# A local-attention layer stack on one core: attention weights turned on VectorE, score heads on partition quarters, group transposes in 64-row pieces, and a new static order

## The chip, the cores and the metric

The program runs on one core of a Trainium2 chip. Its time is the device time of one execution in microseconds (us). Five engines work side by side, each on its own list of instructions in a fixed order: TensorE (PE, with its weight loads PEld), VectorE (DVE), ScalarE (ACT), GpSimd (POOL) and SyncE (SP), which here only issues DMAs. They meet through semaphores that the program waits on.

## The reference

All of it is float32. A short first part (a sequential linear-attention update over 2048 tokens) feeds a stack of six layers on 2048 tokens of 128 features. One layer, shortened:

```python
def attn_layer(x, Wqkv, qs, ksc, Wo):            # x is token-shifted: half the features one token late
    q, k, v = jnp.split(x @ Wqkv, 3, -1)         # 16 heads of 64
    q = l2norm(q) * qs; k = l2norm(k) * ksc
    q = q * cos * scale + rotate_half(q) * sin * scale
    k = k * cos / scale + rotate_half(k) * sin / scale
    sim = einsum('bhwie,bhwje->bhwij', bq, look(bk)) * 8.0   # windows of 32, each sees itself and the one before
    attn = softmax(where(mask, -big, sim), -1)               # 32 queries x 64 keys, per head and window
    return einsum(attn, look(bv)) @ Wo
def ffn_layer(x, g, bln, W1, b1, W2, b2):        # hidden width 341
    a, gate = jnp.split((layernorm(x) * g + bln) @ W1 + b1, 2, -1)
    return a * gelu(gate) @ W2 + b2
for i in range(6):
    x = attn_layer(shift_tokens(x), ...) + x
    x = ffn_layer(shift_tokens(x), ...) + x
```

Layer norms and residual sums stand around both parts.

## The kernel before

**Tiles and steps.** The 2048 tokens are 16 tiles of 128 tokens (4 windows of 32); four tiles are a group. Six layers of 16 tiles are 96 tile visits, `t`. One loop over `s` (0 to 114) is written out for every engine: in iteration `s` each engine does one stage of several visits, `t = s - lag`. Attention goes by tile, the feed-forward part by group (`group_at(s, lag)`: every fourth iteration). The order of the stages inside an iteration is written by hand, engine by engine, and nothing reorders it later.

**One visit on TensorE.** `project` (L254) makes k (n = 2, 3) and later q (n = 0, 1) in the same two PSUM banks `psq`. VectorE applies the rotary tables (L858, L865 for k, L921, L928 for q), ScalarE squares them for the norm (L1148, L1247) and so frees `psq`. `turn` (L264) transposes q and k, in halves of 64 rows, with an identity as moving operand. `mask` (L285) and `scores` (L294) fill `pss`. VectorE takes the row maximum (L874) and subtracts it (L879), ScalarE takes the exponential (L1198), VectorE sums (L954) and inverts (L816), GpSimd multiplies (L1320). The weights `pr` must then be transposed: `turn_p` does it on TensorE, 16 transposes of 64 rows into two banks (L264, with `pr`), and ScalarE copies them to `pT` (L1212, L1219). `values` (L276) makes the value-times-output products U0 to U3, which ScalarE copies to `u4`, and `mix` (L310) weighs them by `pT` into one bank Y, which VectorE adds to the residual (L910).

**The norm's chain.** GpSimd adds the two rotary halves (L1325 for q, L1353 for k). The inverse roots of the sums of squares come by a polynomial: `ssc` (VectorE, L822), `rg`, `ra` (ScalarE), `rb` (GpSimd, L1374), `rs`, `rf` (ScalarE), `rp`, `rn` (GpSimd), and GpSimd scales q and k (L1337, L1341). It also makes the table `tab` of each visit (L1315).

**One group.** SyncE fetches the token-shifted rows (`xf`), VectorE takes statistics (L849, L936), ScalarE normalizes to `xh` (L1169). Four 128x128 transposes F (L667) turn it into one bank, and ScalarE copies with gain and bias to `xnT` (L1241). `hidden` (L324) makes three gate blocks G0 to G2 and three value blocks A0 to A2, `narrow` (L334) the product Z, and four 128x128 transposes X (L657) turn the new residual, which ScalarE copies to `x0S` (L1226, L1227), the input of the next layer.

**PSUM.** `psq` and `pss` take two banks each; the other four are a ring, `take(what, n)`: each result takes the next bank and waits until the use four places before has been copied out.

Of the kernel before, what the change touches and what calls it, by code (L numbers as in the profile page):

```python
# [7 lines left out]
I32 = mybir.dt.int32  # L8
# [36 lines left out]
LOAD_W = 9  # L45
# [19 lines left out]
def build(nc, x_d, wvT_d, w0T_d, bv_d, eta_d, wqk_d, scale_d, mvT_d, wo_d, w1_d, w2_d, par_d,  # L65
          ident_d, rep_d, mask_d, rope_d, kfac_d, level_d, out_d):
    ctx = ExitStack()
    with ctx:
# [101 lines left out]
        def c_u(c):  # L170
# [39 lines left out]
                             "rn_ready", "qn_k", "qn_q"))  # L210
        tab_ready, kprev_ready = sem("tab_ready"), sem("kprev_ready")
# [31 lines left out]
        def _(pe):  # L243
# [15 lines left out]
            def halves_turned(banks, src):  # L259

                for blk in range(8):
                    for r in range(2):
                        rows = slice(64 * r, 64 * r + 64)
                        last = tr(banks[r][:, 64 * blk:64 * blk + 64], src(blk)[rows], ident[rows, rows])  # L264
                        if blk == 7:
                            last.then_inc(filled[ring.index(banks[r])], 1)
# [13 lines left out]
            def mask(t):  # L280

                for w in range(NWIN):
                    for r in range(2):
                        rows = slice(HD * r, HD * r + HD)
                        mm(pss[WIN * w:WIN * w + WIN, 512 * r:512 * r + 512], rep16[rows, WIN * w:WIN * w + WIN],  # L285
                           mask16[rows, int(t % TILES == 0 and w == 0), :], start=True, stop=False)

            def scores(t, half):

                for pair in range(4 * half, 4 * half + 4):  # L290
                    for w in range(NWIN):
                        for r in range(2):
                            rows = slice(HD * r, HD * r + HD)
                            last = mm(pss[WIN * w:WIN * w + WIN, 512 * r + KEYS * pair:512 * r + KEYS * pair + KEYS],  # L294
                                      qT[rows, pair, WIN * w:WIN * w + WIN],
                                      kT[rows, t % 2, pair, WIN * w:WIN * w + KEYS],
                                      start=False, stop=(pair == PAIRS - 1))
# [211 lines left out]
            for s in range(STEPS + 19):  # L509
                t = s - 6  # L510
# [4 lines left out]
                u = unit_at(s, 3)  # L515
                if u >= 0:
                    features(u)
                i = group_at(s, 14)
                if i >= 0:
                    bank, n = take("G0", i)  # L520
                    nbank, m = place["F", i]
                    pe.wait_ge(freed[nbank], m + 1)
                    if i % GROUPS == 0:
                        pe.wait_ge(w1_ready, 16 * (i // GROUPS + 1))
                    wait(pe, freed[bank], n)
                    hidden(ring[bank], 0, 1).then_inc(filled[bank], 1)
# [1008 lines left out]
```

## Time and profile before

| what | us |
|---|---|
| time, median of 3 runs (lowest to highest) | 1578.05 (1576.39 to 1578.88) |
| the profiled execution's own time | 1578.04 |
| its span in the trace | 1576.2 |
| TensorE busy | 1515.7 (96%) |
| VectorE / ScalarE / GpSimd busy | 1210.7 / 1166.0 / 1213.3 |

The profile is of one execution. Its own time is 1.8 us over the span, which runs from the first to the last instruction. "Busy" is the union of an engine's instructions; neighbours overlap a little, so what an instruction costs in a dense row is the distance of the starts, not its duration. Everything below the first 150 us is the steady loop.

### The profile page before, as it was taken

Reading aid. Unit: us, or ns where it says so; the run is one execution under the profiler, and the core shown is the slowest. Engines: PE = TensorE matmul, PEld = TensorE weight load, DVE = VectorE, ACT = ScalarE, POOL = GpSimd, SP = SyncE. Lnnn points to the kernel's source line nnn. Section 1 sums busy time; section 2 is a strip of 40 time slices with the busy share of each in tenths; the row PEclk is TensorE's granted clock in tenths of the full one; section 3 lists DMA queues with packets and bytes.
Section 4 is the critical chain, followed back from the end, with each engine's and each line's share of the span. In section 5 each row is a group of like instructions: output and inputs, shape, how many; then the busy total and the mean of one; then the engine's idle time right before and its main releaser. Section 6 shows DMA issues by size and latency. Waiting matters only on the chain.

```text
span 1576.2 us, 79230 instructions
## 1 busy us (share of the span) xinstructions
PE 1515.7 (96%) x35024; PEld 870.2 (55%) x35024; DVE 1210.7 (77%) x1693; ACT 1166.0 (74%) x2322; POOL 1213.3 (77%) x1051
## 2 busy tenths in 40 slices
PE   7877999999999999999999999999999999999995
PEld 6723555555555555555555555555555555655563
DVE  5478887787787787787787787777877777877853
ACT  4337778778778778778777787787787788788772
POOL 6148988888888788888888878888888888887851
PEclk9968999999999999999999999999999999999998
DMA  5000000100000100000100000100000000000000
GB/s 198 29 1 29 4 10 10 57 10 10 4 23 10 57 10 10 3 19 14 57 10 10 3 19 15 53 13 10 4 18 14 3 10 10 4 19 15 4 17 28
DMA packets 24583, 33.21 MB, mean 21 GB/s; under 512 B 2373, under 2 KB 21425, under 8 KB 23345
## 3 DMA queue, kind: packets, MB, share of 16 engines
q1 hardware_dynamic: 24240, 28.15, 5.5%
q8 instruction: 276, 4.52, 1.2%
q14 instruction: 67, 0.54, 0.1%
HBM read 20.80 MB, written 1.05 MB: 14 GB/s over the span
## 4 chain that ended last, share of the span: by engine, by line
PE 87%; DVE 2%; issue 1%; DMA 1%; ACT 0%; SPq 0%; POOLq 0%; DVEq 0%; POOL 0%; ACTq 0%
PE ring L276 21%; PE psq L254 20%; PE ring L310 11%; PE ring L264 10%; PE pss L294 9%; PE ring L324 7%; PE ring L334 4%; PE pss L285 2%; DMA xf<-x 1%; PE ring L667 1%; PE ring L657 1%; PE ring L347 1%; DVE qb L865 0%; DVE mx L874 0%; DVE ss L901 0%
## 5 line engine op out<-in xcount | busy, mean ns | idle before, releaser
L254 PE MATMUL psq<-wqk,x0S 128*32 128x512 f32 x3072 | 395.5, 605 | 10.5 <-ACT sq L1148 8.0
L276 PE MATMUL ring<-mh,x0S 128*32 128x512 f32 x3072 | 398.3, 595 | 0.7 <-ACT kT L1126 0.7
L1353 POOL TENSOR_TENSOR qa<-qa,qb 128x1024 f32<-128x1024 f32 x96 | 229.3, 2389 | 0.0
L1325 POOL TENSOR_TENSOR qa<-qa,qb 128x1024 f32<-128x1024 f32 x96 | 228.6, 2381 | 0.0
L310 PE MATMUL ring<-u,pT 128*32 128x128 f32 x6144 | 219.6, 274 | 3.8 <-issue 2.9
L858 DVE TENSOR_TENSOR qa<-psq,tab 128x1024 f32<-128x1024 f32 x96 | 117.2, 1221 | 135.5 <-POOL tab L1315 75.0
L310 PEld LDWEIGHTS ring<-u,pT 128*32 128x32 f32 x6144 | 177.6, 110 | 75.7 <-issue 59.7
L254 PEld LDWEIGHTS psq<-wqk,x0S 128*32 128x32 f32 x3072 | 110.8, 111 | 181.1 <-issue 153.9
L1320 POOL TENSOR_TENSOR pr<-pr,rden 128x1024 f32<-128x1024 f32 x96 | 184.0, 1916 | 11.2 <-DVE rden L816 11.2
L1337 POOL TENSOR_TENSOR qa<-qa,rn 128x1024 f32<-128x1024 f32 x96 | 182.8, 1904 | 7.5
L1341 POOL TENSOR_TENSOR qa<-qa,rn 128x1024 f32<-128x1024 f32 x96 | 182.7, 1904 | 0.0
L294 PE MATMUL pss<-kT,qT 64*32 64x64 f32 x12288 | 165.6, 224 | 0.0
L276 PEld LDWEIGHTS ring<-mh,x0S 128*32 128x32 f32 x3072 | 93.4, 109 | 128.0 <-issue 121.4
L962 DVE TENSOR_REDUCE ss<-sq 128x16 f32<-128x1024 f32 x96 | 116.8, 1216 | 56.4 <-ACT sq L1247 56.2
L294 PEld LDWEIGHTS pss<-kT,qT 64*32 64x32 f32 x12288 | 148.2, 105 | 12.9 <-issue 1.4
L1374 POOL TENSOR_TENSOR rb<-ra,ssc 128x32 f32<-128x32 f32 x96 | 24.2, 253 | 166.7 <-ACT ra L1119 166.6
L264 PEld LDWEIGHTS ring<-ident,qa 64*128 64x128 f32 x3072 | 103.4, 139 | 82.8 <-issue 81.9
L324 PE MATMUL ring<-xh,w 128*32 128x512 f32 (+1 forms) x1056 | 136.3, 594 | 1.7 <-ACT xh L1241 1.7
L921 DVE TENSOR_TENSOR qa<-psq,tab 128x1024 f32<-128x1024 f32 x96 | 116.9, 1218 | 20.5 <-PE psq L254 20.5
L1198 ACT ACTIVATE pr<-pr 128x1024 f32<-128x1024 f32 x96 | 101.3, 1056 | 35.6 <-DVE pr L879 35.4
L1148 ACT ACTIVATE sq<-psq 128x1024 f32<-128x1024 f32 x96 | 98.4, 1025 | 39.3 <-DVE qb L865 31.9
L879 DVE TENSOR_TENSOR pr<-pss,mx 128x1024 f32<-128x1024 f32 x96 | 117.6, 1225 | 3.3
(173 smaller groups left out, 2852.4 us busy)
## 6 DMA issues: line engine op xcount, KB each, us to landing
wqk<-in_wqk SPq DMA_DIRECT2D x6, 1024.0 KB, 5.5
mvT<-in_mvT SPq DMA_DIRECT2D x6, 512.0 KB, 3.8
wo<-in_wo SPq DMA_DIRECT2D x6, 512.0 KB, 5.0
xf<-x SPq DMA_DIRECT2D x24, 128.0 KB
xf<-x SPq DMA_DIRECT2D x24, 127.0 KB
rope<-in_rope SPq DMA_DIRECT2D x1, 2048.0 KB, 10.3
w<-in_w SPq DMA_DIRECT2D x6, 341.0 KB, 3.0
xmid<-in_x SPq DMA_DIRECT2D x4, 256.0 KB, 4.3
```

The lines of the kernel that those rows point to most:

```text
L254: last = mm(psq[WIN * w:WIN * w + WIN, 512 * (n % 2):512 * (n % 2) + 512], x0S[:, tile * P + WIN * w:tile * P + WIN * w + WIN], wqk[:, l % ...
L264: last = tr(banks[r][:, 64 * blk:64 * blk + 64], src(blk)[rows], ident[rows, rows])
L276: last = mm(bank[WIN * g:WIN * g + WIN, :], x0S[:, tile * P + WIN * w:tile * P + WIN * w + WIN], mh[:, l % 2, g, :, :].rearrange("p j n -> ...
L294: last = mm(pss[WIN * w:WIN * w + WIN, 512 * r + KEYS * pair:512 * r + KEYS * pair + KEYS], qT[rows, pair, WIN * w:WIN * w + WIN], kT[rows ...
L310: last = mm(bank[WIN * w:WIN * w + WIN, 0:P], pT[:, half, b * P + WIN * w:b * P + WIN * w + WIN], u4[:, slot, v_w, b * P:b * P + P], start ...
L324: last = mm(bank[c:c + m, :], w1[:, col + c:col + c + m], xnT[:, :], start=True, stop=True)
L879: v.tensor_tensor(p4[t % 2], s4, mx[:, :].unsqueeze(2).unsqueeze(3).broadcast_to([P, HEADS, 2, WIN]), ALU.subtract).then_inc(p_shifted, 1)
L1320: g_.tensor_tensor(p4[t % 2], p4[t % 2], rden[:, :].unsqueeze(1).unsqueeze(3).broadcast_to([P, 2, HEADS, WIN]), ALU.mult).then_inc(p_ready, 1)
L1325: g_.tensor_tensor(qa[:, t % 2, 0:1024], qa[:, t % 2, 0:1024], qb[:, 0:1024], ALU.add).then_inc(sum_q, 1)
L1337: g_.tensor_tensor(a3[t % 2][:, 0:16, :], a3[t % 2][:, 0:16, :], rn[:, 0:16].unsqueeze(2).broadcast_to([P, HEADS, HD]), ALU.mult).then_inc ...
L1341: g_.tensor_tensor(a3[t % 2][:, 16:32, :], a3[t % 2][:, 16:32, :], rn[:, 16:32].unsqueeze(2).broadcast_to([P, HEADS, HD]), ALU.mult).then_ ...
L1353: g_.tensor_tensor(qa[:, t % 2, 1024:2048], qa[:, t % 2, 1024:2048], qb[:, 1024:2048], ALU.add).then_inc(sum_k, 1)
```

## The change

It does five things.

1. `turn_p` and its two PSUM banks and ScalarE copies go. VectorE transposes `pr` to `pT` in 32x32 blocks with one instruction per visit (semaphore `pt_ready`).
2. That needs, for each head quarter, the 32 queries of a window on the partitions of a quarter: `scores` puts the pair's number modulo 4 on the quarter of the partitions and the window in the columns (before: the window on the quarter, the pair in the columns). The mask of the first tile follows. Number and shape of the matmuls stay.
3. The group transposes F and X are done as `halves_turned` with 4 blocks: 8 transposes of 64 rows into two banks (before: 4 of 128 rows into one). ScalarE reads them with two instructions instead of one for F, and four of 256 columns instead of two of 512 for X.
4. The order of stages in the loop is new on all four engines, with new lags: k's projection at `s - 0` instead of `s - 1`, `mix` at `s - 5` instead of `s - 6`, q's and k's turns in two different iterations, the group's statistics at lag 9 instead of 10, its transposes F at 12 instead of 13.
5. SyncE fetches `xf` and the feed-forward weights one iteration earlier (lag 8 for 9, `LOAD_W` 8 for 9).

The core of the diff:

```diff
-LOAD_W = 9
+LOAD_W = 8
...
-            def halves_turned(banks, src):
+            def halves_turned(banks, src, blocks=8):
-                for blk in range(8):
+                for blk in range(blocks):
                     for r in range(2):
                         rows = slice(64 * r, 64 * r + 64)
                         last = tr(banks[r][:, 64 * blk:64 * blk + 64], src(blk)[rows], ident[rows, rows])
...
             def scores(t, half):
-                for pair in range(4 * half, 4 * half + 4):
-                    for w in range(NWIN):
+                for w in range(NWIN):
+                    for g in range(4):
                         for r in range(2):
-                            rows = slice(HD * r, HD * r + HD)
-                            last = mm(pss[WIN * w:WIN * w + WIN, 512 * r + KEYS * pair:512 * r + KEYS * pair + KEYS],
-                                      qT[rows, pair, WIN * w:WIN * w + WIN],
+                            rows, pair = slice(HD * r, HD * r + HD), 4 * half + g
+                            col = 512 * r + 256 * half + KEYS * w
+                            last = mm(pss[WIN * g:WIN * g + WIN, col:col + KEYS], qT[rows, pair, WIN * w:WIN * w + WIN],
                                       kT[rows, t % 2, pair, WIN * w:WIN * w + KEYS],
...
-            def turn_p(banks, t):
-                halves_turned(banks, lambda blk: pr[:, t % 2, blk * P:blk * P + P])
...
-                t = s - 6
+                t = s - 5
                 if 0 <= t < STEPS:
                     bank, n = take("Y", t)
                     wait(pe, freed[bank], n)
-                    hbank, m = place["P0", t]
-                    pe.wait_ge(freed[hbank], m + 1)
-                    hbank, m = place["P1", t]
-                    pe.wait_ge(freed[hbank], m + 1)
+                    pe.wait_ge(pt_ready, t + 1)
...
+                i = group_at(s, 12)
+                if i >= 0:
+                    banks = [take("F0", i), take("F1", i)]
+                    pe.wait_ge(xh_ready, i + 1)
+                    halves_turned([ring[bank] for bank, n in banks], lambda blk: xh[:, blk * P:blk * P + P], QUAD)
...
+                t = s - 4
+                if 0 <= t < STEPS:
+                    dve.wait_ge(p_ready, t + 1)
+                    if t >= 1:
+                        bank, n = place["Y", t - 1]
+                        dve.wait_ge(filled[bank], n + 1)
+                    v.transpose(pT[:, :, :].rearrange("p e n -> p (e n)"), pr[:, t % 2, :]).then_inc(pt_ready, 1)
+                t = s - 3
+                if 0 <= t < STEPS:
+                    dve.wait_ge(s_ready, t + 1)
+                    wait(dve, p_shifted, t)
+                    v.tensor_reduce(mx[:, :], s3, AX.X, ALU.max).then_inc(mx_ready, 1)
...
-                    nc.scalar.copy(pT[:, :, :].rearrange("p e (b n) -> p (e b) n", n=P)[:, :, 0:64], ...)
-                    nc.scalar.copy(pT[:, :, :].rearrange("p e (b n) -> p (e b) n", n=P)[:, :, 64:128], ...)
...
-    mask[:, 1, :, :WIN] = -1e30
+    mask[:, 1, ::NWIN, :WIN] = -1e30
```

The order moves as follows. On TensorE, the iteration of a group's Z and X, before (`psq` rows are `project`, here of q; `ring<-w,uT` is Z, `ring<-ident,pr` is `turn_p`, `pss` rows are the mask and the first half of the scores):

```order
L254 MATMUL psq<-wqk,x0S 32x512 [waits sq_k]
L254 MATMUL psq<-wqk,x0S 32x512 x7
L334 MATMUL ring<-w,uT 32x128 [waits freed3,w2_ready]
L334 MATMUL ring<-w,uT 32x128 x47
L264 MATMUL ring<-ident,pr 128x64 [waits freed1,freed0,p_ready]
L264 MATMUL ring<-ident,pr 128x64 x15
L285 MATMUL pss<-mask,rep 32x512 [waits p_shifted]
L285 MATMUL pss<-mask,rep 32x512 x7
L294 MATMUL pss<-kT,qT 32x64 [waits kprev_ready,freed0,freed2]
L294 MATMUL pss<-kT,qT 32x64 x31
```

And now, from k's projection on (`ring<-ident,x0T` is X, `ring<-ident,qa` the turn of k):

```order
L256 MATMUL psq<-wqk,x0S 32x512 [waits sq_q]
L256 MATMUL psq<-wqk,x0S 32x512 x7
L266 MATMUL ring<-ident,x0T 128x64 [waits freed1,freed0,freed2]
L266 MATMUL ring<-ident,x0T 128x64 x7
L266 MATMUL ring<-ident,qa 128x64 [waits freed3,freed2,qn_k]
L266 MATMUL ring<-ident,qa 128x64 x15
L287 MATMUL pss<-mask,rep 32x512 [waits p_shifted]
L287 MATMUL pss<-mask,rep 32x512 x7
L297 MATMUL pss<-kT,qT 32x64 [waits kprev_ready,freed3]
L297 MATMUL pss<-kT,qT 32x64 x31
```

The turn of the weights is gone from in front of the mask; k's projection and k's turn alone stand there now, and X is eight short pieces.

On VectorE, the stretch of one iteration around k's rotation, before (`qa`, `qb` are the rotary products, `mx` and `pr` the softmax's maximum and difference, `rden` the inverse sum):

```order
L816 RECIPROCAL rden<-den 128x16 [waits p_ready,den_ready]
L822 TENSOR_REDUCE ssc<-ss 128x32 [waits rb_ready,ss_q,ss_k]
L842 SCALAR_TENSOR_TENSOR uT<-ring,par,uT 85x512 [waits freed2,filled2]
L858 TENSOR_TENSOR qa<-psq,tab 128x1024 [waits filled1,tab_ready,pk_done]
L865 TENSOR_TENSOR qb<-psq,tab 128x1024 [waits sum_k]
L874 TENSOR_REDUCE mx<-pss 128x16 [waits p_shifted,s_ready]
L879 TENSOR_TENSOR pr<-pss,mx 128x16x2x32 [waits filled2,mx_ready]
L901 TENSOR_REDUCE ss<-sq 128x16 [waits ssc_ready,sq_k]
L910 TENSOR_TENSOR x<-ring,x0T 128x2x64 [waits freed2,filled0]
L921 TENSOR_TENSOR qa<-psq,tab 128x1024 [waits filled3,tab_ready,pq_done]
L928 TENSOR_TENSOR qb<-psq,tab 128x1024 [waits sum_q]
```

And now, from k's rotation to q's and on to the norm's sum:

```order
L945 TENSOR_TENSOR qa<-psq,tab 128x1024 [waits filled3,tab_ready,pk_done]
L959 TENSOR_TENSOR qb<-psq,tab 128x1024 [waits sum_k]
L967 TENSOR_REDUCE ssc<-ss 128x32 [waits rb_ready,ss_q,ss_k]
L976 STREAM_TRANSPOSE pT<-pr 128x1024 [waits filled0,p_ready]
L981 TENSOR_REDUCE mx<-pss 128x16 [waits p_shifted,s_ready]
L814 TENSOR_TENSOR pr<-pss,mx 128x16x2x32 [waits mx_ready]
L823 TENSOR_TENSOR qa<-psq,tab 128x1024 [waits filled3,tab_ready,pq_done]
L839 TENSOR_TENSOR qb<-psq,tab 128x1024 [waits sum_q]
L849 TENSOR_TENSOR x<-ring,x0T 128x2x64 [waits freed2,filled2]
L855 TENSOR_REDUCE den<-pr 128x16 [waits rden_ready,exp_done]
L858 RECIPROCAL rden<-den 128x16 [waits p_ready,den_ready]
L865 TENSOR_REDUCE ss<-sq 128x16 [waits ssc_ready,sq_k]
```

`ssc` moved from the start of the next iteration to just behind k's rotation, the new transpose stands between it and the maximum, and q's rotation follows the difference at once, where one reduction and the residual sum stood before.

## Rows read from the trace of the kernel before

**Rows 1.** the page: engines' busy time, and TensorE's granted clock in 40 slices.
```profile
PE 1515.7 (96%) x35024; PEld 870.2 (55%) x35024; DVE 1210.7 (77%) x1693; ACT 1166.0 (74%) x2322; POOL 1213.3 (77%) x1051
...
PEclk9968999999999999999999999999999999999998
```

**Rows 2.** timeline of VectorE, two reciprocals (L816): start, duration, instruction, [idle before].
```profile
309.10 1.22 DVE L962 TENSOR_REDUCE ss<-sq 128x16 f32<-128x1024 f32 x1 [0.65 <-ACT sq L1247]
310.24 0.24 DVE L816 RECIPROCAL rden<-den 128x16 f32<-128x16 f32 x1
...
1486.48 0.24 DVE L816 RECIPROCAL rden<-den 128x16 f32<-128x16 f32 x1
```

**Rows 3.** windows; columns: stretch, its length, busy PE, PEld, DVE, ACT, POOL, clock, DMA.
```profile
145.57:195.00 49.43, 48.08 (x1195) 25.89 (x1184) 42.38 (x48) 38.53 (x81) 47.49 (x37) 1.00 0.02 4
310.24:1486.48 1176.24, 1174.15 (x27728) 662.51 (x27724) 937.75 (x1189) 927.43 (x1834) 960.72 (x791) 1.00 0.05 15
549.07:786.78 237.71, 237.69 (x5624) 133.82 (x5620) 189.62 (x242) 188.08 (x373) 194.59 (x160) 1.00 0.06 19
1486.48:1532.57 46.09, 45.42 (x1192) 27.74 (x1188) 29.91 (x55) 34.52 (x67) 26.82 (x24) 1.00 0.05 15
1532.57:1576.20 43.63, 27.45 (x464) 15.30 (x456) 16.61 (x58) 12.35 (x20) 7.66 (x11) 0.86 0.08 25
```

**Rows 4.** timeline of TensorE, one iteration without hidden products: start, duration, instruction.
```profile
834.04 1.21 PE L264 MATMUL ring<-ident,qa 64*128 64x64 f32 x32
835.19 0.86 PE L294 MATMUL pss<-kT,qT 64*32 64x64 f32 x64
...
838.61 1.90 PE L254 MATMUL psq<-wqk,x0S 128*32 128x512 f32 x16
840.44 0.71 PE L264 MATMUL ring<-ident,pr 64*128 64x64 f32 x16
841.08 0.41 PE L285 MATMUL pss<-mask,rep 64*32 64x512 bf16 x8
841.31 0.84 PE L294 MATMUL pss<-kT,qT 64*32 64x64 f32 x64
842.08 0.66 PE L657 MATMUL ring<-ident,x0T 128*128 128x128 f32 x4
842.67 2.78 PE L276 MATMUL ring<-mh,x0S 128*32 128x512 f32 x24
```

**Rows 5.** waits, 549.07 to 786.78 us: waiting <- releaser: us in total, times, longest.
```profile
POOL rb L1374 <- ACT ra L1119: 31.1, 16, 3.1
...
DVE qa L858 <- POOL tab L1315: 13.7, 6, 2.6
...
DVE qa L858 <- PE ring L264: 9.0, 6, 1.6
```

**Rows 6.** groups of the span by line: busy us, mean ns, idle before.
```profile
L1247 ACT ACTIVATE sq<-psq 128x1024 f32<-128x1024 f32 x96 | 98.5, 1027 | 17.8 <-DVE qb L928 15.9
...
L1212 ACT COPY pT<-ring 128x512 f32<-128x512 f32 x96 | 56.4, 587 | 47.5 <-PE ring L264 47.4
...
L667 PE MATMUL ring<-ident,xh 128*128 128x128 f32 x96 | 15.7, 286 | 0.0
```

**Rows 7.** groups by line: nearest to VectorE's new instruction.
```profile
L1325 POOL TENSOR_TENSOR qa<-qa,qb 128x1024 f32<-128x1024 f32 x96 | 228.6, 2381 | 0.0
...
L954 DVE TENSOR_REDUCE den<-pr 128x16 f32<-128x1024 f32 x96 | 115.6, 1204 | 0.5 <-ACT pr L1198 0.5
...
L693 DVE MEMSET uT<- 128x512 f32 x1 | 0.5, 485 | 0.1
```

**Rows 8.** groups by line: two more of GpSimd's.
```profile
L1337 POOL TENSOR_TENSOR qa<-qa,rn 128x1024 f32<-128x1024 f32 x96 | 182.8, 1904 | 7.5
...
L1315 POOL TENSOR_TENSOR tab<-rope,qk_scales 128x256 f32<-128x256 f32 x96 | 70.2, 731 | 0.0
...
L1374 POOL TENSOR_TENSOR rb<-ra,ssc 128x32 f32<-128x32 f32 x96 | 24.2, 253 | 166.7 <-ACT ra L1119 166.6
```

More of the change, by code:

```diff
@@ L507, in _ @@
             features(0)
-            for s in range(STEPS + 19):
-                t = s - 6
+            for s in range(STEPS + 20):
+                if chunk_at(s - 1, 1) >= 0:
+                    chain_w(chunk_at(s - 1, 1))
+                i = group_at(s, 14)
+                if i >= 0:
+                    bank, n = take("G2", i)
+                    wait(pe, freed[bank], n)
+                    hidden(ring[bank], 2, 1).then_inc(filled[bank], 1)
+                t = s - 5
                 if 0 <= t < STEPS:
@@ new lines, in _ @@
+                t = s - 0
+                if 0 <= t < STEPS:
+                    if t < TILES:
+                        for u in range(len(UNITS)):
+                            if UNITS[u][0] == t:
+                                cbank, m = place["C", u]
+                                pe.wait_ge(freed[cbank], m + 1)
+                    if t >= TILES and t % QUAD == 0:
+                        for r in range(2):
+                            xbank, m = place["X%d" % r, (t - TILES) // QUAD]
+                            pe.wait_ge(freed[xbank], m + 1)
+                    if t % TILES == 0:
+                        pe.wait_ge(wqk_ready, 16 * (t // TILES + 1))
+                    wait(pe, sq_q, t)
+                    project(t, 2)
+                    project(t, 3).then_inc(pk_done, 1)
@@ L640, in _ @@
+                t = s - 2
+                if 0 <= t < STEPS:
+                    banks = [take("T0", t), take("T1", t)]
+                    pe.wait_ge(qn_k, t + 1)
+                    for bank, n in banks:
+                        wait(pe, freed[bank], n)
+                    turn([ring[bank] for bank, n in banks], t, 8)
                 t = s - 3
@@ new lines, in _ @@
+                i = group_at(s, 9)
+                if i >= 0:
+                    dve.wait_ge(bst_ready, i + 1)
+                    wait(dve, mrs_ready, i)
+                    for k in range(QUAD):
+                        last = v.bn_aggr(mv[:, k, :], bst[:, k, :])
+                    last.then_inc(mv_ready, 1)
+                t = s - 0
+                if 0 <= t < STEPS:
+                    wait(dve, sum_k, t)
+                    v.tensor_tensor(b4[:, 16:32], q4[:, :, ::-1, :],
+                                    tab[:, t % 2, 3, :].rearrange("p (a d) -> p a d", a=2).unsqueeze(1)
+                                    .broadcast_to([P, HEADS, 2, HD // 2]), ALU.mult).then_inc(rope_k, 1)
```

792 lines of the change are left out of this document (375 added, 417 removed).

## The prediction

> **What bounds the kernel now.** I read four views, in this order. First the page's busy times: TensorE is busy 96% of the span, the three others 74 to 77%, and the granted clock is at its full level from the fifth of the 40 slices to the last but one [rows 1]. A share over the whole span mixes start and end in, so next the windows. The loop starts one visit of a tile with each reciprocal on VectorE. The 13th starts at 310.24 and the 92nd at 1486.48 [rows 2]: 79 iterations in 1176.2 us, 14.89 us each, and TensorE is busy 1174.15 of them, 99.8% [rows 3]. In the 16 iterations of one layer (549.07 to 786.78, 14.86 each) TensorE works 237.69 of 237.71 us, GpSimd 194.6, VectorE 189.6, ScalarE 188.1. So in three quarters of the span one microsecond of TensorE work is one microsecond of time, until another engine is full. The first iterations differ: from 145.57 to 195.00 four iterations without feed-forward work take 12.36 each, and GpSimd is busy 47.49 of 49.43 us (96%), nearly as much as TensorE (48.08) [rows 3]. Third, TensorE's timeline for what each piece costs in the dense row, as a distance of starts [rows 4]. Last, the waits: the others' idle time is waiting in fixed order, the most of it GpSimd's for the norm's chain and VectorE's for the table and for k's turn [rows 5].
>
> **The weights' turn.** Removed per visit: 16 transposes on TensorE. Their duration is 0.71 us, but the mask starts at 841.08, 0.64 us behind their start at 840.44 [rows 4]; 0.64 is what goes. Over 79 iterations: 50.6 us. ScalarE loses two copies of 0.59 us a visit (56.4 us for 96 of the first) [rows 6], about 18.8 us per layer; it had no part in the bound, so this pays nothing by itself, but its results come earlier.
>
> **The group's transposes.** Four of 128 rows cost 0.59 us in the row (842.67 less 842.08), F and X alike (15.7 us for 24 F is 0.65 each with its end) [rows 4, 6]. Eight of 64 rows: q's and k's turns are 32 such in 835.19 less 834.04, 1.15 us, so 8 take 0.29. Saved 0.30 each; the stretch has 20 F and about 19 X: 11.7 us. ScalarE's reading grows by one or two small instructions, which its gain covers many times.
>
> **Scores.** Same count, shape and alternation of array parts, only other columns: nothing.
>
> **The transpose on VectorE.** The trace has no such instruction. Bounds for 1024 float32 elements: below, two memsets of 512 at 0.485, about 0.97 us; above, GpSimd's addition of that size, 2.38; nearest is VectorE's own reduction of the same `pr`, 1.20 long, and a new start every 1.14 us (310.24 less 309.10) [rows 2, 7]. I take 1.2 long, 1.14 in the row. (The Trainium skill, "VectorE: DVE Perf Modes", section on the three transpose paths, gives 311 ns for a 128x128 bf16 transpose; no run here shows that, and 896 more elements at an element a cycle would make it an estimated 1.24.) Per layer VectorE goes to 189.6 + 16 x 1.14 = 207.8 us. The layer on TensorE is 237.7 - 16 x 0.64 - 4 x 2 x 0.30 = 225.1. VectorE is 92% full, GpSimd 86%, ScalarE under 78%. So the transpose is hidden, with 1.08 us an iteration to spare; at the upper bound VectorE would need 189.6 + 38.1 = 227.7 and bound the layer itself, 10 us better than now if it never waited.
>
> **Whether the order lets it be hidden.** Behind the transpose stand the maximum, the difference and q's rotation, and on TensorE the mask waits for the difference. It waits for GpSimd's product. From `ssc` that chain is `rb` 0.25, k's sum 2.39, `rp` and `rn` 0.5, `tab` 0.73, two scalings 1.90 each and the product, of the same form, 1.9 [rows 7, 8]: 9.6 us, with 0.8 ahead of it for `rg` and `ra`. The transpose that takes it stands one iteration after that `ssc`: 14.1 + 0.2 later. 3.9 us to spare, and even in an iteration of 12 us 1.8. The second loop is `psq`: q's projection 1.83, two rotations 2.35, square 1.03 [rows 6], k's projection. Between the two projections TensorE now has `mix` twice and U0, U1, some 3.5 us, and group work in three iterations of four: just enough to hide the 3.4. Between k's and q's projection it has k's turn, mask, scores twice, U3, U2, q's turn, 5 us for the same 3.4. VectorE in a light iteration: 10.6 us busy now (42.38 in four [rows 3]) and 11.7 with the transpose, plus two places where one instruction must wait for the end of the one before; I put its light iteration at 12.2. TensorE's light one is 12.02 - 0.64 = 11.4 (48.08 in four), GpSimd's 11.9. So in the one light iteration of four VectorE or GpSimd leads by up to 0.5, and the heavy ones have room. I book 5 us of new stalls over the stretch. K's rotation had waited for `tab` and for a turn, 22.7 us per layer [rows 5]; those were slack, and their going pays only in that VectorE has room for the transpose.
>
> **Start and end.** Iterations before 310.24 are light and GpSimd is at 96%; its work stays. They can gain at most 12.36 less 11.9, and I book 2 us in all. The iterations behind 1486.48 lose four turns and four F, 3 us. The last 43.6 us [rows 3] are one group's latency; unchanged.
>
> **The sum.** 50.6 + 11.7 + 2 + 3 - 5 = 62.3 us off the span of 1576.2: 1513.9. The execution took 1.8 more than its span, and its 1578.04 is the median of the runs, so 1515.7; I say 1516.
>
> **The rivals.**
> 1. *The forecast*: TensorE stays full. Its own range: without the 5 us of stalls and with all of the first iterations' gain 1508, with 0.3 us of stall an iteration instead of 0.06, 1535. Say 1503 to 1535.
> 2. *Half eaten by fixed order*: VectorE at 92% in a fixed list waits at places that the sums do not show. At 0.45 us an iteration on TensorE, 79 x 0.45 = 36 less the 5 booked: 1547. For it: VectorE waits 48 us per layer now and only 17 would be left, so two thirds of the waits must vanish. Against: the largest (`tab`, the turn) are cases of VectorE being early.
> 3. *GpSimd is held up by the transpose*. If both could not use memory at once, GpSimd would lose 1.2 us a visit: 194.6 + 19.2 = 213.8 per layer, still under 225.1, but 13.1 in a light iteration against 12.4 now: + 6 before 310.24, and + 0.9 in 20 of the 79 iterations beside the 5 booked, 13 more, 2 gained at the start not gained: 1537. GpSimd's additions last 2381 on average beside VectorE reductions that read SBUF [rows 7], which shows no hold-up by those. The Trainium skill speaks against the change here ("SBUF — State Buffer", section on the two sides): VectorE and GpSimd share a port pair, locked for a whole instruction when VectorE runs in a two-port mode or has two SBUF inputs. No row shows whether a transpose is such a case; the trace agrees only so far that its one-input reductions are not.
> 4. *Slower*: the transpose waits for the product. It heads VectorE's list, so each microsecond of its wait moves maximum, difference, q's rotation, the square, and with them mask and k's projection. VectorE's iteration is 13.0 (207.8 / 16) plus the wait w; TensorE's is 14.07. From w = 1.1 it costs, from w = 1.9 the kernel is slower than before. At w = 3 an iteration is 16.0, 1.1 over today's: 79 x 1.1 = 87, about 1665 with the start's unchanged time. It needs GpSimd 7 us later than by the chain above, as by a circle (late difference, late exponential, late product). Little speaks for that.
> 5. *All hidden, the light ones too*: TensorE's early iterations reach 11.9 and no stall appears: 1506; it lies in the first one's range.
>
> **Chances.** Forecast with the fifth 0.68, second 0.16, third 0.06, fourth 0.08, and 0.02 for a gain beyond 1500. Range for 8 in 10: from 1500 to 1552, which takes in 1, 2 and 3 nearly whole and leaves the fourth out. An upper-bound transpose (2.38) would give 227.7 per layer plus waits of 5, 233: 1578 less 4.9 layers x 5, about 1553, on the edge. A difference of 0.2% (3 us) is about what a measurement can tell here: faster by more 0.90, within 0.02, slower by more 0.08.
>
> **What would show it.** Right: in the layer's window TensorE over 99% busy with about 225 us for 16 iterations; VectorE 208; the transpose at 1.2 us with almost no idle time ahead of it; GpSimd's additions still 2.38. Wrong: idle time of TensorE before `project` (released by a square) or before the mask (by the difference) is the second; GpSimd additions or scalings with a mean some tenths longer is the third; `pT` waiting on GpSimd's `pr` for over 1 us a visit is the fourth; a transpose far over 1.2 us breaks the hiding at its first term.

## The result and the profile after

| | us |
|---|---|
| after, median of 4 runs (lowest to highest) | 1519.55 (1518.25 to 1520.41) |
| before, beside it on the same chip, 4 runs | 1578.47 (1576.39 to 1580.18) |
| ratio, 95% interval | 0.9627, [0.9615, 0.9639] |
| predicted | 1516 (1500 to 1552) |

The change makes the kernel 3.7% faster. The forecast named the right mechanism and was 3.6 us too low; that it came so near is partly luck, since the terms behind it were off by more, in both directions. All readings of traces are of one execution each, of after the one of 1518.25 us, span 1516.5.

First the page of after: busy times, the clock by slices, and of its groups the transpose and GpSimd's two additions.

```profile
PE 1457.7 (96%) x33664; PEld 799.2 (53%) x33664; DVE 1333.0 (88%) x1789; ACT 1079.3 (71%) x2194; POOL 1209.8 (80%) x1051
...
PEclk9969999999999999999999999999999999999998
...
L1325 POOL TENSOR_TENSOR qa<-qa,qb 128x1024 f32<-128x1024 f32 x96 | 228.9, 2385 | 6.5 <-DVE qb L959 6.5
L1384 POOL TENSOR_TENSOR qa<-qa,qb 128x1024 f32<-128x1024 f32 x96 | 228.4, 2379 | 0.0
...
L976 DVE STREAM_TRANSPOSE pT<-pr 128x1024 f32<-128x1024 f32 x96 | 118.7, 1236 | 2.7 <-POOL pr L1366 2.6
```

TensorE still fills 96% of the span at full clock; VectorE went from 77% to 88%. The transpose lasts 1.236 us and had 2.7 us of idle time ahead of it in all 96 visits: it hardly waits for GpSimd's product. Of GpSimd's two additions (2385 and 2379 ns; 2381 before for the first, [rows 7]) only k's, L1384, runs beside the transpose: in 71 of the 96 visits they overlap, by 0.97 us on average, and there it lasts 2378 ns, against 2381 in the 25 others.

The reciprocals that bound the windows, and one transpose in its row, on VectorE's timeline (start, duration, line, operation):

```profile
300.24 0.25 DVE L858 RECIPROCAL rden<-den 128x16 f32<-128x16 f32 x1
...
592.88 1.25 DVE L976 STREAM_TRANSPOSE pT<-pr 128x1024 f32<-128x1024 f32 x1
594.05 1.19 DVE L981 TENSOR_REDUCE mx<-pss 128x16 f32<-128x1024 f32 x1
...
1427.81 0.25 DVE L858 RECIPROCAL rden<-den 128x16 f32<-128x16 f32 x1
```

The transpose takes 594.05 - 592.88 = 1.17 us of VectorE's row. The same 79 iterations as in [rows 3] are now 1427.81 - 300.24 = 1127.57 us, 14.27 each. Windows of after (length, then busy time of each engine, clock, DMA share): first to 13th reciprocal, 13th to 92nd, 16 iterations of one layer, and what is behind the 92nd in two parts.

```profile
140.98:300.24 159.26, 157.32 (x3736) 81.96 (x3736) 150.00 (x176) 119.10 (x248) 143.88 (x117) 0.99 0.02 7
300.24:1427.81 1127.57, 1125.67 (x26584) 602.63 (x26584) 1034.10 (x1267) 858.14 (x1735) 959.46 (x792) 1.00 0.06 18
473.68:701.87 228.19, 228.19 (x5396) 122.16 (x5392) 209.41 (x257) 174.03 (x353) 194.00 (x161) 1.00 0.07 19
1427.81:1473.41 45.60, 45.60 (x1260) 26.59 (x1248) 35.70 (x55) 31.01 (x60) 27.74 (x24) 1.00 0.03 10
1473.41:1516.50 43.09, 22.53 (x368) 13.51 (x360) 21.39 (x64) 9.58 (x16) 7.16 (x11) 0.85 0.10 32
```

In the layer TensorE works every microsecond of 228.19 (237.69 of 237.71 before); VectorE has 209.41, 92%. The gain of 59.7 us of span by place: 4.6 before the first reciprocal (140.98 against 145.57), 5.4 in the twelve iterations after it (159.26 against 164.67), 48.7 in the 79 iterations (1127.57 against 1176.24), 1.0 behind them (88.69 against 89.72).

TensorE's timeline, an iteration without hidden products and then the two group transposes; each piece costs the distance to the next start:

```profile
589.59 0.71 PE L266 MATMUL ring<-ident,qa 64*128 64x64 f32 x16
590.23 0.41 PE L287 MATMUL pss<-mask,rep 64*32 64x512 bf16 x8
590.46 0.84 PE L297 MATMUL pss<-kT,qT 64*32 64x64 f32 x64
591.23 1.92 PE L278 MATMUL ring<-mh,x0S 128*32 128x512 f32 x16
593.08 0.86 PE L297 MATMUL pss<-kT,qT 64*32 64x64 f32 x64
593.87 0.71 PE L266 MATMUL ring<-ident,qa 64*128 64x64 f32 x16
594.51 1.92 PE L256 MATMUL psq<-wqk,x0S 128*32 128x512 f32 x16
...
633.24 0.46 PE L266 MATMUL ring<-ident,x0T 64*128 64x64 f32 x8
633.54 0.66 PE L266 MATMUL ring<-ident,qa 64*128 64x64 f32 x16
...
640.27 0.46 PE L266 MATMUL ring<-ident,xh 64*128 64x64 f32 x8
```

What the reader is to see: k's turn (589.59) and q's (593.87) cost 0.64 each, where both in one burst had cost 1.15 [rows 4]. X (633.24), beside k's turn, costs 0.30; F (640.27), alone between longer work, 0.39 (its next row, values, starts at 640.66).

Summed over TensorE's whole row in the 79 iterations (each piece's distance to the next start; us):

| pieces | before | after | E3 | E5 | E6 | E7 |
|---|---|---|---|---|---|---|
| 128-row work (project, values, hidden, narrow) | 708.6 | 721.8 | 709.9 | 717.8 | 720.9 | 720.9 |
| mix | 151.7 | 138.4 | 154.0 | 140.0 | 138.4 | 138.4 |
| scores | 125.6 | 125.9 | 123.4 | 131.0 | 125.1 | 123.7 |
| turns of q and k | 90.0 | 100.5 | 93.0 | 111.6 | 101.7 | 100.9 |
| turn of the weights | 50.8 | 0 | 0 | 0 | 0 | 79.8 |
| F and X | 22.9 | 13.1 | 22.9 | 13.1 | 22.3 | 13.1 |
| all, with mask and the merge | 1176.2 | 1127.6 | 1129.9 | 1141.2 | 1136.2 | 1204.7 |

The weights' turn left as forecast (50.8). Turns of q and k grew by 10.5: the second burst. The 128-row work and `mix` exchanged 13: `mix` is that much cheaper and the 128-row work that much dearer, with the order changed around them. The last row has two small pieces besides: the mask and the product of the value and output weights that each layer starts with (`ring<-wo,mvT`). The columns E3 to E7 are experiments.

### The profile page after: what moved, and what is told of

It reads as the page before. It is cut to its first block, busy times and chain, and to the rows that moved or that the text cites. A ratio compares the mean times of both kernels' runs of the same rounds, so it can differ in the third digit from the quotient of the medians.

```text
span 1516.5 us, 76132 instructions
## 1 busy us (share of the span) xinstructions
PE 1457.7 (96%) x33664; PEld 799.2 (53%) x33664; DVE 1333.0 (88%) x1789; ACT 1079.3 (71%) x2194; POOL 1209.8 (80%) x1051
## 4 chain that ended last, share of the span: by engine, by line
PE 85%; DVE 2%; POOL 1%; issue 1%; DMA 0%; ACT 0%; SPq 0%; POOLq 0%; DVEq 0%; ACTq 0%
PE psq L256 21%; PE ring L278 21%; PE ring L308 11%; PE pss L297 9%; PE ring L266 9%; PE ring L322 8%; PE ring L332 4%; PE pss L287 2%; PE ring L345 1%; DMA xf<-x 0%; DVE qa L823 0%; DVE qb L839 0%; POOL qa L1361 0%; POOL pr L1366 0%; DVE mx L981 0%
## 5 line engine op out<-in xcount | busy, mean ns | idle before, releaser
L278 PE MATMUL ring<-mh,x0S 128*32 128x512 f32 x3072 | 408.8, 595 | 0.0
L1325 POOL TENSOR_TENSOR qa<-qa,qb 128x1024 f32<-128x1024 f32 x96 | 228.9, 2385 | 6.5 <-DVE qb L959 6.5
L1384 POOL TENSOR_TENSOR qa<-qa,qb 128x1024 f32<-128x1024 f32 x96 | 228.4, 2379 | 0.0
L308 PEld LDWEIGHTS ring<-u,pT 128*32 128x32 f32 x6144 | 170.9, 110 | 62.1 <-issue 60.5
L308 PE MATMUL ring<-u,pT 128*32 128x128 f32 x6144 | 191.2, 274 | 4.5 <-DVE pT L976 4.5
L256 PEld LDWEIGHTS psq<-wqk,x0S 128*32 128x32 f32 x3072 | 93.9, 111 | 182.4 <-issue 166.1
L1339 POOL TENSOR_TENSOR tab<-rope,qk_scales 128x256 f32<-128x256 f32 x96 | 70.7, 737 | 111.5 <-DVE qb L839 111.5
L322 PE MATMUL ring<-xh,w 128*32 128x512 f32 (+1 forms) x1056 | 150.3, 596 | 1.2 <-ACT xh L1168 1.2
L266 PEld LDWEIGHTS ring<-ident,qa 64*128 64x128 f32 x3072 | 110.9, 139 | 75.1 <-issue 48.2
L266 PE MATMUL ring<-ident,qa 64*128 64x64 f32 x3072 | 136.0, 228 | 2.1 <-POOL qa L1361 1.7
L981 DVE TENSOR_REDUCE mx<-pss 128x16 f32<-128x1024 f32 x96 | 114.9, 1196 | 14.8 <-PE pss L297 14.8
L976 DVE STREAM_TRANSPOSE pT<-pr 128x1024 f32<-128x1024 f32 x96 | 118.7, 1236 | 2.7 <-POOL pr L1366 2.6
```

The lines of the kernel that those rows point to most:

```text
L256: last = mm(psq[WIN * w:WIN * w + WIN, 512 * (n % 2):512 * (n % 2) + 512], x0S[:, tile * P + WIN * w:tile * P + WIN * w + WIN], wqk[:, l % ...
L278: last = mm(bank[WIN * g:WIN * g + WIN, :], x0S[:, tile * P + WIN * w:tile * P + WIN * w + WIN], mh[:, l % 2, g, :, :].rearrange("p j n -> ...
L308: last = mm(bank[WIN * w:WIN * w + WIN, 0:P], pT[:, half, b * P + WIN * w:b * P + WIN * w + WIN], u4[:, slot, v_w, b * P:b * P + P], start ...
L322: last = mm(bank[c:c + m, :], w1[:, col + c:col + c + m], xnT[:, :], start=True, stop=True)
L976: v.transpose(pT[:, :, :].rearrange("p e n -> p (e n)"), pr[:, t % 2, :]).then_inc(pt_ready, 1)
L1325: g_.tensor_tensor(qa[:, t % 2, 1024:2048], qa[:, t % 2, 1024:2048], qb[:, 1024:2048], ALU.add).then_inc(sum_k, 1)
```

## The experiments

Each ratio is to the kernel before, timed beside it on the same chip. E1 to E4 change before, the others change after. The theory: the transpose on VectorE takes away 0.64 us a visit, the two turns in place of one burst cost 0.13 of it, the pieces of 64 rows give back something only where nothing else waits, and TensorE stays full. The rival for the gain: it is the new order that brings it, and the transpose by itself would be held up by VectorE's old list.

**E1: before, with the turns parted.**

```diff
-                (turn of q, T2 and T3)
                 t = s - 4
                 if 0 <= t < STEPS:
                     scores(t, 1).then_inc(s_ready, 1)
+                (turn of q, T2 and T3)
```

> The kernel before, with one edit on TensorE: q's turn (T2, T3) stands behind the second half of the scores instead of in front of it, so that k's and q's turns are two bursts of 16 instead of one of 32. Nothing else moves. Theory (a burst of transposes costs 0.13 to 0.14 us beyond its 0.51, in both kernels: 32 in one piece are 1.14 us from start to next start, 16 are 0.64): 96 x 0.14 = 13 us longer, about 1591 against 1578, and the piece of 16 reads 0.64 before scores and before mix. Rival (the 0.5 us of surplus in the changed kernel's iterations come from waits or from U2 and U3 in front of the scores): no difference, 1578 within 2 us.

Measured: 1582.95 us (1581.62 to 1584.83), ratio 1.0029 [1.0019, 1.0039]. TensorE's timeline of this run, around q's turn:

```profile
838.00 0.86 PE L294 MATMUL pss<-kT,qT 64*32 64x64 f32 x64
838.79 0.71 PE L264 MATMUL ring<-ident,qa 64*128 64x64 f32 x16
839.43 1.08 PE L310 MATMUL ring<-u,pT 128*32 128x128 f32 x32
```

and the window of its 79 iterations:

```profile
310.89:1492.90 1182.01, 1182.01 (x27728) 663.12 (x27724) 938.03 (x1189) 929.76 (x1834) 961.63 (x791) 1.00 0.05 15
```

q's turn is 0.64 here (839.43 - 838.79), k's 0.64: the pair costs 101.4 us in the stretch against 90.0. But 1182.0 is only 5.8 more than before, not 11.4: `mix` is 3.2 cheaper (148.5) when a turn stands ahead of it, scores 2.1. So the second burst is real, and about half of it comes back at the neighbours. The size expected (13) was wrong, and so was the rival that expected no difference.

**E2: before, with F and X in pieces of 64 rows.**

```diff
-                    bank, n = take("X", i)
+                    banks = [take("X0", i), take("X1", i)]
...
-                    for k in range(QUAD):
-                        last = tr(ring[bank][:, k * P:k * P + P], x0T[:, QUAD * (i % GROUPS) + k, :], ident[:, :])
+                    halves_turned([ring[bank] for bank, n in banks], lambda blk: x0T[:, QUAD * (i % GROUPS) + blk, :], QUAD)
```

> The kernel before with the group's transposes F and X in 8 pieces of 64 rows into two banks each, and ScalarE reading them in the smaller pieces; order and attention as before. By the prediction 0.30 us for each of 24 F and 20 X, 13 us less: 1565. By the changed kernel's timeline (X 0.30 and F 0.39 in the place of 0.59 each) 0.29 x 20 + 0.20 x 24 = 10.5 us less, 1567.5. Rival (the ring of four banks now also has to free two more places a group, which stalls TensorE in the old order): no gain or a loss.

Measured: 1575.98 us, ratio 0.9991 [0.9982, 1.0000]: worth nothing, or nearly. TensorE from X to k's projection, then ScalarE beside it:

```profile
840.11 0.46 PE L264 MATMUL ring<-ident,x0T 64*128 64x64 f32 x8
840.51 2.78 PE L276 MATMUL ring<-mh,x0S 128*32 128x512 f32 x24
843.33 1.92 PE L254 MATMUL psq<-wqk,x0S 128*32 128x512 f32 x16
```

```profile
840.61 1.53 ACT L1228 COPY x0S<-ring 64x256 f32<-64x256 f32 x4 [0.32 <-PE ring L264]
842.16 1.02 ACT L1254 ACTIVATE sq<-psq 128x1024 f32<-128x1024 f32 x1
843.08 0.58 ACT L1265 COPY u<-ring 128x512 f32<-128x512 f32 x1
```

The projection of the same iteration in the kernel before:

```profile
845.26 1.90 PE L254 MATMUL psq<-wqk,x0S 128*32 128x512 f32 x16
```

X is 0.40 (840.51 - 840.11; 0.59 before), and F and X together save 7.5 us in the stretch. But the projection needs `psq`, which the square frees, and the square (to 843.18) stands behind X's four copies on ScalarE, 840.61 to 842.14. The projection starts at 843.33, right behind it: 2.82 us after the values product started, against 2.59 (845.26 less 842.67 of [rows 4]) before. It is so in all 19 iterations of the stretch that have an X: 2.82 or 2.83 against 2.60, and each time the projection starts 0.14 us behind the square's end, where before it had 0.27. 128-row work grows by 4.8 us and idle time of TensorE from 2.1 to 2.9 us. So X's saving turned into a wait, and a wait of 0.2 us between two matmuls is hardly seen as idle. F's 3.8 us remain in the trace, whose stretch is 3.6 us shorter; the medians show 1.2 us, with an interval from nothing to 2.8. The rival's number held, but by the square and not by the ring of banks that it named.

**E3: before, with the transpose on VectorE and the scores' layout, in the old order.** The transpose stands behind the sum of the weights, where VectorE has `pr` of the visit before.

```diff
-                    turn_p([ring[bank] for bank, n in banks], t)
...
             (VectorE, behind the sum L954)
...
+                    v.transpose(pT[:, :, :].rearrange("p e n -> p (e n)"), pr[:, t % 2, :]).then_inc(pt_ready, 1)
```

> The kernel before with the weights' turn on VectorE and the scores' new layout, everything else in the old order; the transpose stands behind the sum L954. k's and q's turns stay one burst of 32. Theory (TensorE is the only bound, the old order has room for the transpose as well, and nothing is split): 96 x 0.64 = 61 us less, 1517. Rival (the new order was what made room: VectorE's 48 us of waits per layer are not slack in the old order): TensorE idle between instructions, 1535 or more.

Measured: 1528.74 us (1526.40 to 1529.95), ratio 0.9685 [0.9672, 0.9698]. The window of its 79 iterations:

```profile
311.23:1441.16 1129.93, 1126.46 (x26460) 624.09 (x26464) 1022.91 (x1268) 851.43 (x1675) 962.75 (x791) 1.00 0.05 16
```

46.3 us are gone in the stretch of the 50.8 that the turn had cost. So five sixths of the gain (3.15% of 3.73%) come from this edit alone, and the rival falls: VectorE, busy 1022.9 of 1129.9 us in its old list, still hides the transpose. TensorE is idle 3.5 us of the stretch, and 3.4 of them are gaps put down to issue (see E9), not waits for VectorE. The time lies between the two numbers expected, 1517 and 1535. What is missing to 50.8: the turns of q and k are 3.0 dearer, `mix` 2.3, 128-row work 1.3, and scores 2.2 cheaper.

**E4: E3 with the pieces of E2.**

> The kernel before with both of the above, the weights' turn on VectorE and F and X in 64-row pieces, in the old order. Theory: 1578 - 61 - 10.5 = 1507, faster than the changed kernel's 1519.5, since the old order keeps k's and q's turns together. Rival as for the kernel with the transpose alone: 1525 or more.

Measured: 1528.94 us (1523.86 to 1532.77), ratio 0.9686 [0.9665, 0.9707], the stretch 1129.5. As in E2, the pieces bring nothing in the old order, though ScalarE has lost the two `pT` copies: behind an X the projection again starts 2.80 to 2.83 us after the values product, 0.14 us behind the square's end. The theory's 1507 missed; the rival's number, 1525 or more, was met, but by this wait and not by VectorE.

**E6: after, with F and X whole.** The edit is that of E2 turned round.

> The changed kernel with F and X as four whole 128-row transposes into one bank, as before, in the new order. Theory (in the new order the square behind which the old order lost the gain stands in front of X's copies, so the small pieces' gain is paid out in full): 0.29 x 20 + 0.19 x 24 = 10.4 us more, 1530. Rival (as in the old order the small pieces are worth 1 to 2 us): 1521.

Measured: 1530.11 us (1529.31 to 1531.31), ratio 0.9705 [0.9691, 0.9720]. The theory's 1530 was met. The pieces are worth 10.6 us in the new order and 1.2 or nothing in the old one (E2, E4). In the stretch it is 8.7: F and X grow by 9.2 (13.1 to 22.3). In the new order X stands ahead of k's turn, and no projection waits for a square behind its copies. So new order and pieces together give the last 9 us of the gain (1528.7 to 1519.6), and neither gives them alone: with the transpose on VectorE in all of them, the order and no pieces make 1530.1, the pieces and no order 1528.9.

**E8: after, with the transpose done twice.**

```diff
+                    v.transpose(pT[:, :, :].rearrange("p e n -> p (e n)"), pr[:, t % 2, :]).then_inc(pt_first, 1)
+                    dve.wait_ge(pt_first, t + 1)
                     v.transpose(pT[:, :, :].rearrange("p e n -> p (e n)"), pr[:, t % 2, :]).then_inc(pt_ready, 1)
```

> The changed kernel with VectorE's transpose done twice each visit, the second when the first has ended (same result). VectorE's work per layer goes from 209.4 to about 230 us where the layer takes 228.2. If its idle time is slack that can be used in full (the prediction's reading): 230 per layer, about 10 us more in all, 1530. If the fixed order makes it wait at places of its own, which is the prediction's second rival: about 1.3 us for each of the iterations in which the transpose stands in front of the critical maximum and rotation, 96 x 1.0 or more, 1600 and above.

Measured: 1545.56 us (1544.36 to 1548.18), ratio 0.9805 [0.9789, 0.9820].

```profile
309.68:1451.40 1141.72, 1130.10 (x26616) 601.72 (x26616) 1116.61 (x1345) 851.87 (x1735) 959.03 (x792) 1.00 0.06 18
```

VectorE is busy 1116.6 of 1141.7 us, 98%, and the stretch is 14.2 us longer; the iterations before it lost 9.4 (13th reciprocal at 309.68 against 300.24). The time lies between the two numbers expected (1530, and 1600 and above), nearer to the first: most of VectorE's idle time can be used, but not all of it. A transpose of about 2.4 us, the upper bound of the prediction, would thus have cost 26 us and left the kernel 2% faster than before.

**E7: after's order, with the weights' turn on TensorE as before** (16 transposes ahead of q's turn, two ring banks more, copies on ScalarE, and the scores and the mask laid out as before).

> The changed kernel with the weights turned on TensorE again (old layout of the scores, two banks, two copies on ScalarE), directly in front of q's turn, so that both are one burst of 32. It is the new order and the 64-row pieces of F and X without the transpose on VectorE. Theory: 1.14 in the place of 0.64 a visit, 96 x 0.50 = 48 us more, 1567, 10 under the kernel before. Rival (the new order was made for VectorE's transpose, and ScalarE's two copies or the ring of four banks now hold mix up): 1580 or more.

Measured: 1611.48 us (1609.27 to 1614.56), ratio 1.0227 [1.0210, 1.0245]. Of the waits of TensorE in its 79 iterations (total, times, longest):

```profile
PE ring L266 <- ACT u L1149: 22.2, 76, 0.3
```

The weights' turn costs 79.8 us there, 1.01 a visit in place of 0.64, with a wait for a ring bank that ScalarE had not yet copied out in 76 of 79 visits. The rival of this run was right: with the turn on TensorE the new order is worse than the old one, by 2.3%. At this place of the turn, at least; others weren't tried.

**E5: after, with both turns in one stretch of short matmuls**, by moving U3 and U2 (and their copies) behind q's turn. It was meant to win the 10 us of the second burst back.

> The changed kernel with U3 and U2 moved behind q's turn, on TensorE and with their copies on ScalarE, so that k's turn, mask, both halves of the scores and q's turn stand in one block and U2 no longer stands in front of the scores. Theory (leaving U2 or a projection for 64-row work costs 0.13 and 0.09 us on TensorE, in the changed kernel's timeline 1.855 against 1.72 for 16 matmuls): 0.14 x 96 = 13 us less, 1506. Rival (q's turn, now 1.85 us earlier, waits for GpSimd's scaling of q, which ends 2.9 us before it in the trace, or mix waits for U3's copy): no gain or a loss, with idle time of TensorE.

Measured: 1537.46 us (1530.89 to 1539.50), ratio 0.9744 [0.9719, 0.9769]: 18 us slower than after. Scores still stand between the turns. TensorE is idle 23.1 us of its stretch of 1141.2 (1.9 of 1127.6 in after). Without its idle time the stretch is 1118.1 us, 7.6 less than after's 1125.7: the move does save work, if less than expected, and the gaps cost nearly three times as much. Its longest waits in the whole span, and one of them in the timeline:

```profile
PE ring L266 <- issue: 14.8, 12, 2.9
PE pss L297 <- issue: 11.4, 14, 3.3
```

```profile
772.51 0.71 PE L266 MATMUL ring<-ident,qa 64*128 64x64 f32 x16
773.15 0.41 PE L287 MATMUL pss<-mask,rep 64*32 64x512 bf16 x8
773.38 1.46 PE L297 MATMUL pss<-kT,qT 64*32 64x64 f32 x128
774.77 0.34 PE L266 MATMUL ring<-ident,qa 64*128 64x64 f32 x4
777.98 0.86 PE L266 MATMUL ring<-ident,qa 64*128 64x64 f32 x12 [2.87 <-issue]
```

In mid-turn, after 4 of its 16 transposes, TensorE stops for 2.87 us without waiting for any semaphore. Behind the first 130 us there are 27 waits put down to issue, 26.8 us together (2 in after, 1.9 us). 22 of them stand 135 to 176 matmuls into a run of short matmuls (k's turn, mask, scores, q's turn) that the move had made, 168 long, or 176 behind an X; the other five stand elsewhere, so that what is expected of E9 below says too much of them. After's longest such run is 88, or 96 behind an X. The rival's number (no gain or a loss) was met, by gaps that it didn't name. Two more kernels test whether the length of the run is the cause.

**E9: after, with the first half of the scores issued twice** (run of 152 short matmuls), and **E10: half of each half twice** (runs of 120 and 112; the same work). Each run that begins with an X is 8 longer. The scores issued twice come out doubled.

```diff
 (E9)
                     scores(t, 0)
+                    scores(t, 0)
 (E10, and the same for scores(t, 1))
+                    scores(t, 0, range(2))
                     scores(t, 0)
```

> The changed kernel with the first half of the scores issued twice in place (those scores come out doubled): 64 more 64-row matmuls in every visit, so that turn of k, mask and scores make one unbroken run of 152 short matmuls (88 in the changed kernel), and the second half of the scores with the turn of q one of 80, as before. It looks at the stalls of the run that put the two U behind q's turn: 27 gaps for which the profile names no cause, all 126 or more short matmuls into a run of 168. By the theory that TensorE's supply of instructions runs short in a long run, the gaps come back: 10 to 20 us of idle time put down to issue in the span, beside 96 x 0.78 = 75 us of added work (a pair of half-scores behind another costs about 0.78): 1519.5 + 75 + 10 to 15 = 1604 to 1610. By the rival, that those stalls came from the order of the waits of q's turn and ScalarE, no such gap: under 3 us put down to issue, 1594.

> The changed kernel with half of each half of the scores issued twice in place (those scores come out doubled): again 64 more short matmuls per visit, but spread so that the runs are 120 and 112 long. Both see the same work as in the run with 152 and 80. If the length of a run decides, nearly no gap put down to issue here (under 4 us in the span) and about 1519.5 + 75 = 1595; if the mean density of instructions decides, the same gaps as there, 1604 to 1610.

Measured: E9 1628.58 us (1624.07 to 1630.24), ratio 1.0315 [1.0293, 1.0337]; E10 1601.52 (1599.34 to 1604.88), ratio 1.0154 [1.0135, 1.0173]. TensorE's longest waits of E9, one of them in its timeline, and those of E10:

```profile
PE pss L297 <- issue: 19.4, 33, 2.2
...
PE ring L278 <- issue: 7.7, 9, 2.6
```

```profile
874.30 0.71 PE L266 MATMUL ring<-ident,qa 64*128 64x64 f32 x16
874.94 0.41 PE L287 MATMUL pss<-mask,rep 64*32 64x512 bf16 x8
875.17 1.43 PE L297 MATMUL pss<-kT,qT 64*32 64x64 f32 x125
877.61 0.30 PE L297 MATMUL pss<-kT,qT 64*32 64x64 f32 x3 [1.02 <-issue]
877.84 1.50 PE L278 MATMUL ring<-mh,x0S 128*32 128x512 f32 x12
```

```profile
PE pss L297 <- issue: 11.8, 23, 1.7
...
PE ring L308 <- issue: 2.1, 1, 2.1
```

The gaps came back without any move: behind the first 130 us 30.8 us in E9 (46 gaps) and 15.3 in E10 (27), against 1.9 in after. The rival for E5 (waits of q's turn and ScalarE) falls as the main cause. Length decides in part: the same work in runs of 152 and 80 costs 27 us more than in runs of 120 and 112. But E10 was expected under 4 us of gaps, and its time lies between the two numbers expected (1595, and 1604 to 1610), so length alone is not the rule; more short matmuls in an iteration bring gaps too. And E9 is 19 us over its range: its stretch grew by 1.16 us an iteration, 0.92 of it in the scores with their gaps, 0.23 in the 128-row work behind them, where stalls and gaps follow too.

What TensorE waits for in these gaps can be read from the DMA queues. The page lists one of kind "instruction", queue 8 (packets, MB, share of the DMA engines; after, then E9):

```profile
q8 instruction: 265, 4.34, 1.2%
...
q8 instruction: 313, 5.13, 1.3%
```

E9 has 6144 matmuls more than after (39808 against 33664), each with its weight load, and 48 packets more: 256 instructions of TensorE to a packet of 16,384 bytes. All 102 gaps put down to issue behind the first 130 us (27 in E5, 46 in E9, 27 in E10, 2 in after) stand at the same place of this count: the number of TensorE's instructions ahead of the gap is a multiple of 256 and 193 to 195 more. Each gap ends 1.15 to 1.66 us after the packet whose turn it is has landed, and where there is no gap, TensorE reaches that place never sooner than 1.20 us after the landing. In the gap of 2.87 us above, the packet ran from 775.50 to 776.56, and TensorE went on at 777.98. So in these gaps TensorE waits for its own instructions. In the median of each trace a packet starts when TensorE has 207 to 232 instructions left before it needs it, that is 104 to 116 matmuls with their loads; from the packet's start to the end of a gap it is 2.2 to 3.0 us. By the rows above, 64 score matmuls take 0.79 us, so 104 of them an estimated 1.3 us: too short for the packet. That is why a long run of short matmuls opens gaps, why the gap can come early in a run or just behind it, and why E10, with shorter runs but as many short matmuls, has some too.

The two longest gaps of E5 (3.3 us up to 313.5 and 2.9 up to 778.0) stand where a layer's weights come in. What the DMA engines moved in E5 around the second, 760 to 790 us in 40 slices of 0.75 us (busy tenths, then GB/s):

```profile
DMA  0010000010000002798992167997000000010000
GB/s 0 0 22 0 0 0 0 0 22 0 0 0 0 0 0 49 246 395 249 288 309 64 33 120 254 416 423 247 21 33 22 33 0 0 0 22 0 0 0 0
```

The gap, 775.1 to 778.0, is in slices 21 to 24 (309, 64, 33 and 120 GB/s), between the two bursts of that load. In both gaps the packet started only when TensorE had already stopped, 0.8 and 0.4 us into the gap, and then took 1.1 us, no longer than others. So beside a load the packet may start late; all six gaps of over 2 us in E5, E9 and E10 have such traffic, but most of the shorter ones have none. Why it starts late is not shown.

## Why the prediction was right, and where its terms were off

1. **The bound** was right. TensorE was full before and is full now, 228.19 of 228.19 us in a layer, where 225.1 was forecast.
2. **The weights' turn**, 50.6 us: 50.8 left the row, and E3 by itself gives 46.3 in the stretch. Right.
3. **"0.64 is what goes" per visit** is the step that failed. It holds for the weights' turn, but the new order also splits the burst of q and k, which the prediction itself had read as 1.15 for 32 transposes, and never priced as 2 x 0.64. That is +10.5 us in the row; E1 shows that with its neighbours it nets about 6 in the old order.
4. **The group's transposes**, 0.30 each: X gave 0.29, F 0.20. The price of 0.29 for eight pieces was taken from a burst of 32; alone between long matmuls eight such cost 0.39. F and X fell from 22.9 to 13.1, 9.8 us instead of 11.7. E6 confirms it whole (10.6); E2 and E4 show that it needed the order, which the sum did not say: in the old one the square stood behind X's copies.
5. **The transpose on VectorE**: 1.24 long and 1.17 in the row, where 1.20 and 1.14 were taken. Right, and hidden: 2.7 us of waiting for the product over 96 visits. The estimate of 1.24 us worked out from the Trainium skill, "VectorE: DVE Perf Modes", section on the three transpose paths, agrees with the measured 1.236.
6. **Stalls of 5 us** did not come: TensorE is idle 1.9 us of the 1127.6 (2.1 before). The stretch by its row: 50.8 for the weights' turn, 9.8 for the pieces, less 10.5 for the second burst and 1.4 for all the rest, 48.7 in place of 57.3.
7. **Start** 2 us: 10.0. 4.6 of them before the first reciprocal, which the prediction left out: k's projection comes one iteration earlier, and VectorE's first rotation for k starts at 81.14 us (before: 86.81). It comes with the new order: that reciprocal starts at 140.6 to 143.3 us in the seven kernels that have it and at 145.6 to 147.9 in the five that don't; which of its moves does it was not tested. The twelve iterations after it gave 5.4, where 12.36 less 11.9 had allowed 5.5 and 2 were booked. **End** 3 us: 1.0, and why isn't shown. Start and end made up for two thirds of what the stretch fell short of its 57.3, so the total is nearer than its terms, and that is luck.
8. **The rivals.** Half eaten by VectorE's order: E3 shows VectorE hiding it even in the old list. GpSimd held up by a port: k's addition lasts 2378 ns beside a transpose and 2381 without one, and in E8, with 1.9 us of transposes beside it in 92 visits, 2383, so the lock that "SBUF — State Buffer" of the Trainium skill tells of (section on the two sides) didn't show here. The transpose waiting for the product: 2.7 us in all. None took part.

Open: why `mix` costs 0.17 us an iteration less in after (138.4 against 151.7 us, with 128-row work dearer by as much). The traces show that a piece's distance depends on its neighbours, not why; and why a packet of instructions starts late beside a load.

## What to carry to other kernels

Where one engine is full and another has room, work taken from the first can be worth nearly its distance of starts in the dense row: here 46.3 of 50.8 us in the old fixed list of the second engine as well. Price the new order too, though: each burst that it splits costs its own start, a shortened piece pays only if what follows isn't waiting for something else, and two edits can be worth 10 us together and nothing apart. Long runs of very short matmuls have a limit of their own, since TensorE's instructions must arrive in time: spread them between longer work, and when a gap has no semaphore, look at the instruction queue.

## What the runs showed of the hardware

- A VectorE transpose in 32x32 blocks of 128x1024 float32 takes 1.236 us and didn't slow GpSimd's addition beside it (2378 ns with it, 2381 without).
- 16 transposes of 64x64 float32 on TensorE between other work take 0.64 us of its row, 32 in one burst 1.14 to 1.15; 8 take 0.30 ahead of a turn of 16 and 0.39 to 0.40 between other work, four of 128x128 0.59.
- 16 values matmuls of 128 rows take 1.72 us of the row ahead of more 128-row work (587.76 - 586.04 in after's timeline) and 1.85 ahead of scores (593.08 - 591.23).
- TensorE's instructions come in packets of 256 (16,384 bytes) on a DMA queue of their own. Where short matmuls use them up before the next packet is there, TensorE stops for 0.15 to 3.3 us with no semaphore waited for, and goes on 1.15 to 1.66 us after the landing: 1.9 us of such gaps with runs of 88 and 80 short matmuls, 15 with 120 and 112, 31 with 152 and 80, 27 with 168.
